# Routed experts of a mixture layer: tiles of twelve slots worked in halves, in place of tiles of eight slots worked whole

## The reference

```
rw = softmax(router_logits)                  # (128, 8): one row of logits for each batch row
w, sel = top_k(rw, 2);  w = w / w.sum()      # two experts for each batch row
def mlp(x, gate_w, up_w, down_w):            # gate, up: 128 x 512, down: 512 x 128
    g = x @ gate_w;  u = x @ up_w
    return (gelu(g) * u) @ down_w
for e in range(8):
    out += dense_w[:, e] * mlp(x, skill_gate[e], skill_up[e], skill_down[e])
out += mlp(x, shared_gate, shared_up, shared_down)
```

## Time and profile before

| | |
|---|---|
| median of 3 runs | 423.44 us |
| profiled execution, its time | 420.41 us |
| its span in the profile | 418.5 us |
| tiles, first to last matmul of their gate rows' start | 94.33 to 244.62 us |
| TensorE, VectorE, ScalarE, GpSimd busy | 362.9, 339.5, 283.9, 213.9 us |

### The profile page before, as it was taken

The page is one execution under the profiler, slowest core; times in us unless marked ns, Lnnn a source line. Parts: engine busy times, 40 slices in busy tenths (PEclk is TensorE's granted clock), DMA queues, the critical chain, the costliest instruction groups (busy, mean ns, idle before and its releaser), DMA issues.

```text
span 418.5 us, 7530 instructions
## 1 busy us (share of the span) xinstructions
PE 362.9 (87%) x2316; PEld 312.6 (75%) x2316; DVE 339.5 (81%) x698; ACT 283.9 (68%) x347; POOL 213.9 (51%) x423
## 2 busy tenths in 40 slices
PE   5897977999999999999999999999999974003997
PEld 3575764769999999999999997677767752001797
DVE  3486557985989898998899899966658899979894
ACT  3465776957677676666766674455557799999750
POOL 2367654899644535444453102332248168994352
PEclk9996998999999999999999999999999999555999
DMA  8889874766666676667767506000000000000022
GB/s 265 312 283 353 305 247 151 232 217 260 216 256 241 229 276 212 269 226 246 258 226 270 212 0 188 17 0 2 1 0 2 0 0 1 0 2 0 1 102 100
DMA packets 22160, 64.64 MB, mean 154 GB/s; under 512 B 3043, under 2 KB 9190, under 8 KB 17510
## 3 DMA queue, kind: packets, MB, share of 16 engines
q1 hardware_dynamic: 20646, 63.94, 43.3%
q10 hardware_dynamic: 1472, 0.20, 0.3%
HBM read 49.88 MB, written 12.58 MB: 149 GB/s over the span
## 4 chain that ended last, share of the span: by engine, by line
PE 62%; DVE 16%; POOL 7%; ACT 7%; issue 5%; DMA 2%; POOLq 1%; DVEq 0%; ACTq 0%
PE ps L334 61%; DVE S L674 6%; PE ps L331 2%; POOL WD L1377 2%; DVE O_i L671 1%; DVE Hl L665 1%; DVE G L665 1%; DMA wscr<-wst 1%; POOL Hl L1377 1%; ACT ps L1146 1%; DVE HbS L665 1%; ACT U L1146 1%; ACT xnT L1146 1%; DMA S<-in_cond_dram 1%; DVE S L665 1%
## 5 line engine op out<-in xcount | busy, mean ns | idle before, releaser
L334 PE MATMUL ps<-xg,Wr 128*128 128x256 f32 x864 | 109.6, 283 | 0.1
L1455 POOL CAST xg<-XT 128x64 fp32r x288 | 74.1, 309 | 67.0 <-PE ps L334 67.0
L334 PEld LDWEIGHTS ps<-xg,Wr 128*128 128x128 f32 x864 | 106.2, 192 | 0.6 <-POOL xg L1455 0.6
L1146 ACT ACTIVATE Gb<-ps 128x1024 f32<-128x1024 f32 (+1 forms) x68 | 56.0, 824 | 41.2 <-PE ps L334 41.0
L665 DVE TENSOR_TENSOR HbS<-Gb,ps 128x1024 f32<-128x1024 f32 (+1 forms) x68 | 65.7, 968 | 19.1 <-PE ps L334 15.5
L1146 ACT ACTIVATE Hh<-HbS 128x1024 fp32r<-128x1024 f32 (+1 forms) x68 | 58.2, 855 | 29.8 <-DVE HbS L665 29.7
L671 DVE SCALAR_TENSOR_TENSOR C<-ps,Wt,C 128x32 f32 x288 | 56.1, 276 | 10.3 <-PE ps L334 10.0
L665 DVE TENSOR_TENSOR Hl<-HbS,Hh 128x1024 fp32r<-128x1024 f32 (+1 forms) x53 | 57.7, 1088 | 1.3 <-ACT Hh L1146 1.1
L1377 POOL TENSOR_TENSOR Hl<-HbS,Hh 128x512 fp32r<-128x512 f32 x15 | 19.8, 1318 | 53.3 <-ACT Hh L1146 53.2
L334 PE MATMUL ps<-XT,SHh 128*128 128x512 f32 x128 | 45.7, 399 | 0.4 <-DVE XT L665 0.4
L334 PE MATMUL ps<-Hh,WT 128*128 128x256 f32 x288 | 40.4, 283 | 0.0
(11 more groups left out here) (202 smaller groups left out, 691.9 us busy)
## 6 DMA issues: line engine op xcount, KB each, us to landing
Wr<-wscr SPq DMA_DIRECT2D x36, 1024.0 KB, 4.9
wscr<-wst SPq DMA_DIRECT2D x16, 512.0 KB, 4.6
stg<-n_L_cond_skill_gate_dram SPq DMA_DIRECT2D x8, 256.0 KB, 5.7
stg<-in_L_cond_skill_up_dram SPq DMA_DIRECT2D x8, 256.0 KB, 6.1
wdr<-n_L_cond_skill_down_dram SPq DMA_DIRECT2D x8, 256.0 KB, 5.1
xscr<-X SPq DMA_DIRECT2D x8, 256.0 KB, 4.8
X<-xscr SPq DMA_DIRECT2D x8, 256.0 KB, 4.9
out_dram<-X SPq DMA_DIRECT2D x7, 256.0 KB, 2.0
```

The source lines that it names most:

```text
L334: return e.matmul(o_, l, r, start=start, stop=stop, skip_group_check=True)
L1146: return e.activation(o_, i_, func, **kw)
L1455: last = e.tensor_copy(xg[:, i % XR, :, T * s:T * s + T].rearrange("p a t -> p a t"), XT[:, :, :, bass.ds(regs[s], 1)].rearrange("p a t o ...
```

## The change

A tile has twelve slots, 384 columns, and 24 tiles are always run. Each tile is worked in two halves h = 2i and 2i+1. A half is two of the four blocks of hidden channels: 6 gate and 6 up matmuls of 384 columns. Their results take turns in three pairs of banks (0 and 1, 2 and 3, 6 and 7). `down(h)` is 6 matmuls and stands behind `unit(h + 2)`, not behind the next tile's unit. VectorE makes the low part of even halves, and GpSimd that of odd halves, ahead of each fetch from the fifth on. The scatter of a tile is cut into four slots and eight slots. `C` has 140 columns for each token in place of 136.

```diff
-SL = 8
-NT = 39
-NM = 36
+SL = 12
+NT = 28
+NM = 24
...
+        def blocks(x):
+            b = (0, 2, 6)[x % 3]
+            return ps[:, 512 * b:512 * b + 1024].rearrange("p (u n) -> p u n", u=2)[:, :, 0:HW]
...
+        def low_of_half(h):
+            if h >= 2 * NM:
+                return d_ehl, h - NM + 1
+            return (k_ehl if h % 2 else d_ehl), h // 2 + 1
...
-            def unit(i):
+            def unit(h):
+                i, e_ = h // 2, h % 2
...
+                    elif m == 0:
+                        w.wait_ge(d_eh, h - 1)
+                    else:
+                        w.wait_ge(a_eg, h)
...
-                    for q in range(4):
...
+                    for u in range(2):
+                        cs = slice(128 * (2 * e_ + u), 128 * (2 * e_ + u) + 128)
+                        o_ = blocks(2 * h + m)[:, u, :]
...
+            def down(h):
+                i, e_ = h // 2, h % 2
+                if e_ == 0:
...
+                        w.wait_ge(d_ey, i - 1 if i < NM else i)
...
+            for h in range(2 * NM + 2):
+                if h < 2 * NM:
...
+                    unit(h)
                 else:
...
+                    shared_up(HK + h - 2 * NM)
+                if h >= 2:
+                    down(h - 2)
...
+            def hidden_of(h):
+                w.wait_ge(p_eu, h + 1)
+                w.wait_ge(a_eg, h + 1)
+                if h >= 2:
+                    w.wait_ge(*low_of_half(h - 2))
...
-            for i in range(NM + 1):
-                if i >= 2:
-                    scatter(i - 2)
-                if 1 <= i:
-                    low_of(i - 1)
-                if i < NM:
-                    hidden_of(i)
-                else:
-                    for n in range(HK, HK + 2):
-                        shared_hidden(n)
-            scatter(NM - 1)
+            for h in range(2 * NM + 4):
+                if h < 2 * NM:
+                    hidden_of(h)
+                elif h < 2 * NM + 2:
+                    shared_hidden(HK + h - 2 * NM)
+                if h >= 4:
+                    scatter(h // 2 - 2, *((4, SL) if h % 2 else (0, 4)))
+                if h < 2 * NM and h % 2 == 0:
+                    low_of(h)
...
+            for h in range(2 * NM):
+                gelu_of(h)
+                if h % 2 == 0:
+                    down_weights(h // 2)
+                high_of(h)
...
-            for i in range(XR, NM):
-                fetch(i)
+            for i in range(NM):
+                h = 2 * i + 1
+                w.wait_ge(a_ehh, h + 1)
+                low(two(HLf, place_h(h)), two(HbSf, place_b(h)), two(HHf, place_h(h))).then_inc(k_ehl, 1)
+                if i + XR < NM:
+                    fetch(i + XR)
```

More of the change, by code:

```diff
@@ L20 @@
 E = 8
-SL = 8
-NT = 39
-NM = 36
+SL = 12
+NT = 28
+NM = 24
 NSLOT = SL * NT
 XR = 4
-DW = 136
+DW = 140
 RM = 12582912.0
 J0 = 2
+HW = SL * T
 class Waits:
@@ L260, in place @@
         def place(n):
-            return (n if n < HK else n + 2) % 4
+            return (n if n < HK else 3 - n) % 4
         def half(q, h):
@@ L525, in unit @@
                     last.then_inc(done, 1)
[L527 to L533, removed]
-                    for a in range(2):
[L535 to L539, removed]
+            def down(h):
+                i, e_ = h // 2, h % 2
+                if e_ == 0:
+                    if i == 0:
+                        w.wait_ge(a_sy, J0)
+                    elif i == 1:
+                        w.wait_ge(d_xt, 8)
+                    else:
+                        w.wait_ge(d_ey, i - 1 if i < NM else i)
+                    w.wait_ge(a_wt2, i + 1)
+                Z = BY[pair(i)][:, 0:HW]
+                w.wait_ge(a_ehh, h + 1)
+                for u in range(2):
+                    ws = slice(128 * (2 * e_ + u), 128 * (2 * e_ + u) + 128)
+                    for a in range(2):
+                        mm(Z, WT[:, i % 2, a, ws], two(HHf, place_h(h))[:, u, :], e_ + u + a == 0, False)
+                w.wait_ge(*low_of_half(h))
+                for u in range(2):
+                    ws = slice(128 * (2 * e_ + u), 128 * (2 * e_ + u) + 128)
+                    last = mm(Z, WT[:, i % 2, 0, ws], two(HLf, place_h(h))[:, u, :], False, e_ + u == 2)
                 last.then_inc(p_ed, 1)
@@ L568, in _ @@
                     w.wait_ge(s_wz[r], 16)
-                    unit(i)
-                    w.wait_ge(d_ey, i)
-                    down(i)
+                    for h in (2 * i, 2 * i + 1):
+                        unit(h)
+                    for h in (2 * i, 2 * i + 1):
+                        down(h)
                 w.wait_ge(d_ey, NT)
@@ L925, in _, with low_of, scatter @@
             tiles = e.value_load(etI[0:1, 0, NT:NT + 1], min_val=0, max_val=NT * 512)
[L927 to L938, removed]
+            def hidden_of(h):
[3 more added lines that the diff above has]
+                    w.wait_ge(*low_of_half(h - 2))
+                if h >= 2 * NM:
+                    w.wait_ge(*low_of_half(h - 1))
+                tt(two(HbSf, place_b(h)), two(Gbf, 0), blocks(2 * h + 1), MUL).then_inc(d_eh, 1)
+            def low_of(h):
+                w.wait_ge(a_ehh, h + 1)
+                low(two(HLf, place_h(h)), two(HbSf, place_b(h)), two(HHf, place_h(h))).then_inc(d_ehl, 1)
+            def scatter(i, a, b):
                 w.wait_ge(d_tab, 3)
                 at_ = nc.values_load_multi_w_load_instructions(
-                    colI[0:1, SL * i:SL * i + SL], engines=(mybir.EngineType.DVE,), min_val=0, max_val=DW - 1, skip_runtime_bounds_check_because=WHY)[1]
-                w.wait_ge(p_ed, i + 1)
+                    colI[0:1, SL * i + a:SL * i + b], engines=(mybir.EngineType.DVE,), min_val=0, max_val=DW - 1, skip_runtime_bounds_check_because=WHY)[1]
+                w.wait_ge(p_ed, 2 * i + 2)
                 w.wait_ge(s_zero, 16)
@@ L947, in scatter @@
                     w.wait_ge(d_ey, i)
-                for s in range(SL):
-                    c = spot(at_[s])
+                for s in range(a, b):
+                    c = spot(at_[s - a])
                     last = stt(c, BY[pair(i)][:, T * s:T * s + T], Wt[:, SL * i + s:SL * i + s + 1], c, MUL, ADD)
-                last.then_inc(d_ey, 1)
+                if b == SL:
+                    last.then_inc(d_ey, 1)
             Sb = S4[:, 0:36]
@@ L1251, in _, with gelu_of, high_of @@
             tiles = e.value_load(etI[0:1, 0, NT:NT + 1], min_val=0, max_val=NT * 512)
[L1253 to L1261, removed]
+            def gelu_of(h):
+                w.wait_ge(p_eg, h + 1)
+                w.wait_ge(*((d_eh, h) if h else (d_sh, HK)))
+                do(two(Gbf, 0), blocks(2 * h), ACT.Gelu_apprx_tanh).then_inc(a_eg, 1)
+            def high_of(h):
+                w.wait_ge(d_eh, h + 1)
+                w.wait_ge(*((p_ed, h - 2) if h >= 3 else (p_sd, h + 6)))
+                do(two(HHf, place_h(h)), two(HbSf, place_b(h))).then_inc(a_ehh, 1)
             def down_weights(i):
@@ L1273, in down_weights @@
                 else:
-                    w.wait_ge(p_ed, i - 1)
+                    w.wait_ge(p_ed, 2 * i - 2)
                 do(WT[:, i % 2, :, :], WD[:, :, bass.ds(at_, 512)]).then_inc(a_wt2, 1)
[L1277 to L1286, removed]
+            for h in range(2 * NM):
+                gelu_of(h)
+                if h % 2 == 0:
+                    down_weights(h // 2)
+                high_of(h)
+            for n in range(HK, HK + 2):
+                shared_gelu(n)
+            w.wait_ge(p_ed, 2 * NM - 2)
+            shared_high(HK)
             passed = dict(w.passed)
```

94 lines of the change are left out of this document (48 added, 46 removed).

## The result

The changed kernel takes 429.28 us, median of 4 runs (428.69 to 429.51), against 423.63 (422.42 to 423.87) for the kernel before in the same session. The ratio is 1.0184, interval 1.0131 to 1.0236: slower, by 1.3 to 2.4%. (The two medians alone divide to 1.0133, the lower end of this.) The forecast of 421.7 and its range up to 426.8 are wrong.

What follows compares the result with a forecast made beforehand. TensorE was taken to bound the kernel, by matmul count times distance. Terms -5.2 (matmuls) + 0.95 (start) + 1.1 (first tiles) + 1.4 (end) = -1.75 us gave a forecast of 421.7 us, range 418.0 to 426.8.

Steps and rivals of the forecast that it cites:

- The matmuls: TensorE in the tiles: 864 matmuls of 384 columns at 0.174 us replace 1296 at 0.120, -5.2 us (-6.9 to 0.0).
- The middle: In the steady tiles TensorE stays without a gap despite GpSimd's new work: 0 us, at most 2.4 in all.
- The halfway values: Durations at 768 elements, between rows at 512 and 1024: hidden product 0.95, GpSimd's low part 1.84, high part 0.84, gelu 0.81 us.
- rival B: In the steady tiles GpSimd becomes the pace at 6.5 us a tile, +5.8 us, total 427.5 us; chance 0.14.
- C: TensorE's matmul distance at 384 columns is 180 ns, so the matmul term is 0, total 426.9 us; chance 0.04.
- D: In the tiles VectorE's chain exceeds its 0.7 us to spare; TensorE waits 0.1 us a tile, 424.1 us; chance 0.14.
- The beginning: Before the first unit, four more GpSimd copies in the first fetch start TensorE 0.95 us later, at 95.28.
- The waits at the first tiles: TensorE waits 1.2 us for GpSimd's first low part and 0.4 for late slot additions; less 0.5 earlier losses, net +1.1.
- The end: Behind the tiles, twenty slot additions on VectorE delay block 9's low part; TensorE waits 1.4 us (0 to +2.5).

Runs made afterwards that it cites:

- six: Changed kernel with VectorE's untaken body cut to two extra tiles, and three fetches instead of four ahead of GpSimd's first low part: 420.32 us, ratio 0.9959.
- twelve: The kernel of seven, with the low parts of odd halves also on VectorE and none on GpSimd: 421.57 us, a single execution.
- experiment five: Changed kernel with VectorE's untaken body cut to two extra tiles, and tile 22's eight additions ahead of block 9's hidden product: 420.77 us, ratio 0.9967.
- one: The short body: changed kernel with VectorE's untaken body cut to two of four further tiles, 58 rows instead of 116: 423.82 us, ratio 1.007.
- two: Kernel before, with VectorE's untaken body made of seven tiles' instructions in place of three, 133 rows for 57: 426.33 us, ratio 1.0154.
- nine: Changed kernel with the edits of experiment five and six, all four further tiles, additions of tiles 26 and 27 on GpSimd (VectorE 66 rows): 420.04 us, ratio 0.9944.
- ten: Changed kernel with VectorE's whole untaken body of four tiles (116 rows), plus the reordering of experiment five and the fetches of six: 424.36 us, ratio 1.0063.
- three: Changed kernel with VectorE's untaken body split into two adjacent `If`s of two tiles each, nothing left out: 429.08 us, ratio 1.017.
- eleven: Changed kernel with three of the four further tiles in VectorE's untaken body, 87 rows: 420.22 us, a single execution.
- seven: Changed kernel with VectorE's untaken body cut to two extra tiles, plus the reordering of experiment five and the fetches of six: 420.22 us, ratio 0.9938.
- eight: Kernel before with only the larger tables, 336 slots and `C` of 140 columns: 421.12 us, ratio 0.9952.

## Why the prediction was wrong

**The matmuls, -5.2 forecast, -4.5 measured.** Right in kind. A half takes 176.63 - 173.48 = 3.15 us for 18 matmuls, 174.8 ns each; 864 x 0.1748 = 151.0 against 155.5.

**The middle, 0 forecast, 0 measured.** TensorE is busy 40.00 of 40. Durations, by form in the changed kernel:

```profile
L702 DVE TENSOR_TENSOR HbS<-Gb,ps 128x768 f32<-128x768 f32 x48 | 45.8, 953 | 29.2 <-PE ps L363 25.6 <-ACT Gb L1188 3.3 <-issue 0.2
L1420 POOL TENSOR_TENSOR HLf<-HbS,HHf 128x768 fp32r<-128x768 f32 x24 | 44.4, 1852 | 28.0 <-ACT HHf L1188 28.0
...
L1188 ACT ACTIVATE HHf<-HbS 128x768 fp32r<-128x768 f32 x48 | 40.7, 848 | 37.6 <-DVE HbS L702 37.2
L1188 ACT ACTIVATE Gb<-ps 128x768 f32<-128x768 f32 x48 | 39.0, 813 | 13.1 <-PE ps L363 13.1
```

The halfway values 0.95, 1.84, 0.84 and 0.81 held within 1%. GpSimd waits 0.84 us a tile where I had 0.5, since its low part and its copies took 1.85 + 3.65 = 5.5 us and not 5.7, so rival B is out; rivals C and D are out with the distance and with 40.00 of 40.

**The beginning.** From GpSimd's first copy to the first unit it was 94.33 - 91.42 = 2.91 us; now the copies start at 94.25 and the unit at 98.11, 3.86 us: 0.95 more, as forecast. It holds beside the chance in the start itself: 2.9 to 3.0 us in all four traces with eight copies a fetch, 3.9 in eight of the ten with twelve; six and twelve took 4.4 and 4.3. The waits at the first tiles are 0.75 and 0.56 (forecast 1.2 and 0.4). Taking them away gave 155.90 - 154.05 = 1.85 us, with smaller waits among them, against 1.6 gross forecast.

**The end, without the jump, +1.4 forecast.** With the short body the wait is 1.78 us and the stretch 19.37 - 17.58 = 1.8 longer. Right, and experiment five gave 1.3 of it back.

**The step that failed is one that the working does not have.** "The end" counts VectorE's operations from the last slot addition to block 10's hidden product and puts nothing between them. The sum took the untaken `If` for free, as it had been: in the earlier trace rows the eight additions from 253.64 on and the product at 255.15 join without a gap. The diff showed `NT - NM` going from 3 to 4 and `SL` from 8 to 12: VectorE's body grew from 57 rows to 116, and I never counted rows that are not executed. That cost 4.96 us on VectorE, 6.71 - 1.78 = 4.9 more on TensorE and, with the lower clock behind it, 26.10 - 19.37 = 6.7 us of the stretch.

Sum as measured: -4.5 + 0.95 + (1.9 - 0.5) + 1.8 + 6.7 = +6.3 us, of which +6.7 is the jump. The medians differ by 5.7, the ratio gives 7.8. Without the jump the terms come to -0.4, 1.4 worse than the -1.75 forecast, half of it by the first term.

**What is shown and what is not.** Shown: the length of code passed over decides (one, two, nine against ten), the second of two adjacent jumps pays in place of the first (three), and at this branch it is a step between 87 and 116 rows (eleven). Where the branch stands in its block of code was not varied, so another branch may have its step elsewhere.

Argued, not shown, is why. A packet of 8192 bytes of code starts inside the gap wherever there is one, and the engine goes on 1.8 to 1.9 us behind it. The later the packet, the longer the gap: 2.47, 2.89, 3.02 and 3.31 us after the branch in two, three, ten and the changed kernel, with 4.30, 4.73, 4.86 and 5.18 us to the next instruction. The packet alone proves little: in both traces of the kernel before, in one, in five to nine and in eleven one starts 2.4 to 3.6 us after the branch too, when VectorE has long gone on, and the profile does not tell which engine it is for. That VectorE waits for this packet is the reading that fits all traces. The Trainium skill, "Runtime: NRT & Kernel Launch", section "Instruction fetch mechanics", says that code is fetched ahead in order only, and that a taken branch to a target outside what is held forces a fetch before the engine can go on. The traces agree. The page gives no price; here it is 4.3 to 5.2 us from branch to next instruction. The same page puts the blocks at 16 KiB; the packets here have 8192 bytes.

Open: how much of the 5 us comes from the DMA engines being full at that time (0.85 busy in 255 to 260 us, by `X<-xscr`); no run moved those loads. Full DMA engines alone do not make the gap: in eleven they are 0.95 busy from 255 to 257 us, around its branch at 255.707, and the jump takes 0.23 us. Open too is the short body's ratio of 1.007 where the terms come to -0.4 us. (To the 0.9938 of seven it is 5.6 us, where the traces give 2.4 in the tiles and 1.3 behind them; the two ratios were taken on different chips.) Start times went from 93.61 to 99.93 us over the ten executions of the changed kernel and its variants, which is more than this difference.

## What to carry to other kernels

Before trusting an untaken `If` as free, count the instructions in its body on each engine, not only those that run, and look for the last place where the critical engine jumps. If the body must be long, spread it over engines that wait at that place anyway, as nine does. Putting the jump where its engine has time should do as well; no run tried it. Of a change that makes the body of a loop or tile larger, ask what of it stands in code for the rare case.

## What the runs showed of the hardware

- The jump over 58, 66 and 87 rows took 0.23 us each between branch and next instruction, over 116 rows 5.18, 4.86 and, as two jumps, 4.73 us; over 133 rows in the kernel before 4.3.
- In ten, where TensorE waited 5.28 us, the granted clock of 255 to 260 us was 0.52 (the 1.2 GHz level for nearly all of it). In two, with a wait of 2.82 us, it was 0.72 in 260 to 265 us. After 1.78 us it kept 1.00:

```profile
260.00:265.00 5.00, 3.39 (x15) 2.79 (x16) 4.91 (x10) 1.86 (x3) 1.30 (x1) 1.00 0.78 268
```

  That is the short body around its wait at 261.61. A long wait is paid for a second time: 2.4 us beside 4.6 in ten against nine.
- 384 columns cost 174.8 ns a matmul, 14.8 beside the columns at 2.4 GHz (160.0); 256 have 13.3 beside them (12.4 in eight) and 512 have 14.2.
